# Flamingo stack, two layers, one core: layer 0's scores and values for eight heads in one visit, with a new order of the steps

## What is computed

```
x = x + tanh(g_xattn[0]) * xattn0(layernorm(x), ctx)   # 16 heads of 64
x = x + tanh(g_ffn[0])   * ffn0(layernorm(x))          # 8 experts, gate by softmax and threshold
x = x + tanh(g_xattn[1]) * xattn1(layernorm(x), ctx)   # 16 heads of 16
x = x + tanh(g_ffn[1])   * ffn1(layernorm(x))          # top 2 of 8, first two batches' 512 tokens

xattn0:  q = (x @ Wq.T).reshape(b, nq, H, DH);  k, v likewise from ctx
         sim  = einsum('bihd,bjhd->bhij', q, k) * SCALE
         attn = softmax(sim)
         out  = einsum('bhij,bjhd->bihd', attn, v) @ Wo.T + bo
```

## Time and profile before

| | |
|---|---|
| median of 3 runs | 3825.88 us |
| lowest to highest | 3822.79 to 3827.25 us |
| the profiled execution | 3827.74 us |
| its span, first to last instruction | 3826.0 us |
| mean granted PE clock over the span | 0.985 |
| PE busy | 3723.1 us (97%) |
| DVE busy | 2669.2 us (70%) |
| ACT busy | 1749.8 us (46%) |
| POOL busy | 1340.4 us (35%) |

### The profile page before, as it was taken

One profiled execution on the slowest core, in us unless ns is written; L12 is line 12 of the kernel. 1 busy time (PEld: TensorE's weight loads), 2 busy tenths in 40 slices (PEclk: granted clock), 3 DMA queues, 4 the chain that ended last, 5 costly groups with the idle time before them and its releaser, 6 DMA issues.

```text
span 3826.0 us, 96464 instructions
## 1 busy us (share of the span) xinstructions
PE 3723.1 (97%) x34836; PEld 2979.5 (78%) x34836; DVE 2669.2 (70%) x5726; ACT 1749.8 (46%) x3369; POOL 1340.4 (35%) x1301
## 2 busy tenths in 40 slices
PE   6999999999999999999999999999999999999959
PEld 4787878878878878787887887887888788788745
DVE  4676776777677677677777767767767777776646
ACT  4445445444444444544544444444454454444411
POOL 3334333333333433433333343343343333334300
PEclk8999999999999999999999999999999999999969
DMA  2000000000000000000000000000000000000001
GB/s 90 14 17 9 15 16 10 14 16 13 11 16 13 12 15 16 9 15 16 11 13 16 13 11 16 13 12 15 16 9 15 16 12 13 16 13 11 13 29 55
DMA packets 58914, 64.80 MB, mean 17 GB/s; under 512 B 5344, under 2 KB 55808, under 8 KB 58240
## 3 DMA queue, kind: packets, MB, share of 16 engines
q10 hardware_dynamic: 34688, 32.52, 2.9%
q1 hardware_dynamic: 24192, 31.81, 2.5%
HBM read 47.01 MB, written 17.30 MB: 17 GB/s over the span
## 4 chain that ended last, share of the span: by engine, by line
PE 84%; DVE 11%; issue 2%; POOL 2%; DVEq 1%; ACT 1%; DMA 0%; POOLq 0%; SPq 0%; ACTq 0%
PE g L693 25%; PE g L699 14%; PE scores L693 10%; PE scores L795 6%; PE g L853 6%; DVE xn L1048 4%; PE g L762 4%; PE g L862 3%; PE scores L846 3%; DVE y_nm L1126 3%; PE scores L827 3%; PE g L713 3%; PE scores L799 2%; PE g L773 1%; POOL y_rstd L437 1%
## 5 line engine op out<-in xcount | busy, mean ns | idle before, releaser
L623 ACT ACTIVATE prob<-scores 120x1024 f32<-120x1024 f32 x512 | 510.2, 1022 | 499.0 <-PE scores L799 327.4
L1187 DVE SCALAR_TENSOR_TENSOR x<-g,lg_w,x 128x256 f32<-128x256 f32 x1024 | 483.4, 482 | 61.1 <-PE g L693 36.1
L490 POOL TENSOR_TENSOR q_lo<-an,q_hi 128x512 fp32r<-128x512 f32 x256 | 328.5, 1284 | 341.3 <-ACT q_hi L654 341.3
L541 ACT CAST q_hi<-g 128x512 fp32r<-128x512 f32 x256 | 150.0, 586 | 582.7 <-PE g L693 582.6
L693 PE MATMUL g<-ew_hi,yT_hi 128*128 128x512 f32 x1024 | 412.3, 403 | 0.0
L693 PE MATMUL g<-ew_lo,yT_hi 128*128 128x512 f32 x1024 | 401.8, 392 | 0.0
L693 PE MATMUL g<-ew_hi,yT_lo 128*128 128x512 f32 x1024 | 399.9, 390 | 0.0
L435 POOL TENSOR_TENSOR y_rstd<-y_mv,eps 128x2 f32<-128x2 f32 x128 | 25.0, 195 | 1051.1 <-DVE y_mv L1043 1051.1
L1126 DVE TENSOR_REDUCE x_nm<-g 128x4 f32<-128x480 f32 x512 | 310.5, 648 | 102.3 <-PE g L762 102.3
L1126 DVE TENSOR_REDUCE y_nm<-g 128x4 f32<-128x480 f32 x512 | 301.0, 650 | 109.5 <-PE g L773 109.5
L1091 DVE TENSOR_TENSOR an<-g,inv 128x512 f32<-128x512 f32 x256 | 176.5, 690 | 239.3 <-ACT inv L644 155.7
(11 more groups left out here) (209 smaller groups left out, 9900.4 us busy)
## 6 DMA issues: line engine op xcount, KB each, us to landing
x_in<-in_x ACTq DMA_DIRECT2D x64, 256.0 KB, 2.9
out<-y_x SPq DMA_DIRECT2D x64, 256.0 KB, 2.1
ctx_in<-in_ctx ACTq DMA_DIRECT2D x128, 120.0 KB, 2.5
wk_s<-in_gu SPq DMA_DIRECT2D x8, 512.0 KB, 3.5
wk_s<-in_wk SPq DMA_DIRECT2D x1, 1024.0 KB, 5.1
prob<-in_wq SPq DMA_DIRECT2D x1, 1024.0 KB, 7.7
wv_s<-in_wv SPq DMA_DIRECT2D x1, 1024.0 KB, 10.3
vx<-in_wo SPq DMA_DIRECT2D x8, 128.0 KB, 7.9
```

The lines of the kernel that those rows point to most:

```text
L490: g.tensor_tensor(q[1][:, 2 * h:2 * h + 2, :], an[:, 2 * (h % 2):2 * (h % 2) + 2, :], q[0][:, 2 * h:2 * h + 2, :].bitcast(F32), ALU.subtra ...
L541: a.copy(dst, ring.bank(job)[:, 0:cols]).then_inc(done.sem, 1)
L623: a.activation(prob[:, e % 2].rearrange("p o u s -> p (o u s)"), scores[0:NK, banks, :].rearrange("p o c -> p (o c)"), ACT.Exp, scale=scal ...
L1187: ins = v.scalar_tensor_tensor(out=x1[:, t, :], in0=ring.bank(Y_FFN[j])[:, o * D:(o + 1) * D], scalar=lg_w[:, t, 2 * n + o:2 * n + o + 1], ...
```

## The change

A visit of `x_st` now makes the scores of two quads (eight heads): the first quad of the pair goes to banks 0 and 1 of `scores`, the second to banks 2 and 3. There are two visits instead of four. A visit of `x_pv` makes the sums of eight heads into one ring bank and then the values of its two quads into two further ring banks, so it has three jobs in the ring. The two visits of ACT to invert work on 512 columns each, read the sums from the ring bank and empty it. `pv` is no longer used for the sums. The ring has 56 jobs instead of 54 in a round, so the bank of nearly every job moves. `ORDER` is new throughout.

```diff
-            each = {"n_max": 2, "y_max": ROWS4}.get(name, 1)
+            each = {"n_max": 2, "y_max": ROWS4, "x_pv": 3}.get(name, 1)
...
-X_PV = [("x_pv", g) for g in range(QUADS)]
+X_SUM = [("x_pv", 3 * h) for h in range(2)]
+X_PV = [("x_pv", 3 * (g // 2) + 1 + g % 2) for g in range(QUADS)]
...
+            def x_st(i, h):
+                for g in (2 * h, 2 * h + 1):
+                    x_scored.wait(act, i, g + 1)
+                    if h == 1:
+                        ring.full(act, i, X_PV[g - 2])
+                    exp(g, slice(2 * (g % 2), 2 * (g % 2) + 2), SCALE0, x_probs)
...
+            def x_pv(i, h):
+                ring.full(act, i, X_SUM[h])
+                ring.has_emptied(a.activation(inv[:, h, :], ring.bank(X_SUM[h])[:], ACT.Ln), X_SUM[h])
+                ring.empty(act, i, X_SUM[h])
+                a.activation(inv[:, h, :], inv[:, h, :], ACT.Exp, scale=-1.0).then_inc(x_recip.sem, 1)
...
+                if h == 1:
+                    x_probs.wait(pe, i, 2)
+                for g in (2 * h, 2 * h + 1):
+                    x_qlo.wait(pe, i, g + 1)
+                    scores_of_quad(g, lambda rows, p: both(kT, rows, p, ALL),
+                                   lambda rows, p: both(q, rows, p, ALL), x_nmT).then_inc(x_scored.sem, 1)
...
+                x_probs.wait(pe, i, 2 * h + 2)
+                ring.to_fill(pe, i, X_SUM[h])
+                for u in range(2):
                     for j in range(4):
+                        ins = t_.matmul(ring.bank(X_SUM[h])[32 * j:32 * j + 32, u * S:(u + 1) * S], ones[0:NK, :],
+                                        prob[:, u, j % 2, j // 2, :], start=True, stop=True)
+                ring.has_filled(ins, X_SUM[h])
+                for g in (2 * h, 2 * h + 1):
+                    ring.to_fill(pe, i, X_PV[g])
```

The head of the order, from the first step of a round, before and after:

```diff
-    ("x_st", 0), ("y_k", 0), ("y_ffn", 0), ("n_load", 0), ("z_hi", 1), ("n_stat", 0), ("y_ffn", 1), ("n_norm", 0),
+    ("n_load", 0), ("x_st", 0), ("z_hi", 1), ("y_v", 0), ("y_ffn", 0), ("x_st", 1), ("x_pv", 0), ("n_stat", 0),
+    ("y_ffn", 1), ("x_mul", 0), ("x_hi", 0), ("x_mul", 1), ("n_norm", 0), ("y_ffn", 2), ("y_ffn", 3), ("y_ffn", 4),
...
```

More of the change, by code:

```diff
@@ L50 @@
 ORDER = (
-    ("x_st", 0), ("y_k", 0), ("y_ffn", 0), ("n_load", 0), ("z_hi", 1), ("n_stat", 0), ("y_ffn", 1), ("n_norm", 0),
[L52 to L60, removed]
+    ("n_load", 0), ("x_st", 0), ("z_hi", 1), ("y_v", 0), ("y_ffn", 0), ("x_st", 1), ("x_pv", 0), ("n_stat", 0),
+    ("y_ffn", 1), ("x_mul", 0), ("x_hi", 0), ("x_mul", 1), ("n_norm", 0), ("y_ffn", 2), ("y_ffn", 3), ("y_ffn", 4),
+    ("x_hi", 1), ("y_ffn", 5), ("y_ffn", 6), ("y_ffn", 7), ("n_tr", 0), ("y_stat3", 0), ("x_mul", 2), ("x_pv", 1),
+    ("x_hi", 2), ("y_norm3", 0), ("x_mul", 3), ("y_k", 0), ("n_ctx", 0), ("y_res", 0), ("x_hi", 3), ("z_out", 0),
+    ("p_load", 0), ("y_tr3", 0), ("n_k", 0), ("y_q", 0), ("n_k", 1), ("x_out", 0), ("y_max", 0), ("x_out", 1),
+    ("x_out", 2), ("y_max", 1), ("x_out", 3), ("p_stat", 0), ("p_norm", 0), ("n_q", 0), ("n_q", 1), ("y_maxt", 0),
+    ("y_maxt", 1), ("n_q", 2), ("n_q", 3), ("n_max", 0), ("p_tr2", 0), ("y_st", 0), ("n_max", 1), ("p_gate", 0),
+    ("n_max", 2), ("n_v", 0), ("p_lg", 0), ("n_maxt", 0), ("y_st", 1), ("y_pv", 0), ("y_mul", 0), ("n_max", 3),
+    ("p_wt", 0), ("n_v", 1), ("y_pv", 1), ("n_maxt", 1), ("y_mul", 1), ("p_ctx", 0), ("n_res", 0), ("p_eb", 0),
+    ("y_hi", 0),
 )
@@ L228, in flamingo_stack @@
         prob = prob_rows[0:NK]
-        an, inv = sb("an", [P, 4, S]), sb("inv", [P, 2, S])
+        an, inv = sb("an", [P, 4, S]), sb("inv", [P, 2, 2 * S])
         x1 = sb("x1", [P, T, D])
@@ L794, in scores_of_quad @@
                             rows = slice(64 * o, 64 * o + 64)
-                            t_.matmul(scores[0:NK, o, cols], keys(rows, p)[a], queries(rows, p)[b],
+                            t_.matmul(scores[0:NK, 2 * (g % 2) + o, cols], keys(rows, p)[a], queries(rows, p)[b],
                                       start=a + b == 0, stop=False)
@@ L798, in scores_of_quad, with x_st @@
                         rows = slice(64 * o, 64 * o + 64)
-                        ins = t_.matmul(scores[0:NK, o, cols], ident_r[rows, p:p + 1].broadcast_to([64, NK]),
+                        ins = t_.matmul(scores[0:NK, 2 * (g % 2) + o, cols], ident_r[rows, p:p + 1].broadcast_to([64, NK]),
                                         nmT[rows, :], start=False, stop=True)
                 return ins
-            def x_st(i, g):
+            def x_st(i, h):
                 if first(i):
@@ L833, in y_st, with x_pv @@
                 ins.then_inc(y_scored.sem, 1)
-            def x_pv(i, g):
-                x_probs.wait(pe, i, g + 1)
-                if g == 0:
+            def x_pv(i, h):
+                if h == 0:
                     if first(i):
@@ L869, in x_out @@
                 if c == 0:
-                    x_logged.wait(pe, i, 3)
+                    x_probs.wait(pe, i, QUADS)
                 if first(i):
@@ L1087, in x_mul @@
                 ring.full(dve, i, X_PV[g])
-                x_recip.wait(dve, i, g + 1)
+                x_recip.wait(dve, i, g // 2 + 1)
                 if g >= 2:
```

45 lines of the change are left out of this document (8 added, 37 removed).

## The result

The changed kernel takes 3866.2 us (median of four runs, 3863.0 to 3866.4), the kernel before 3826.6 us beside it: a ratio of 1.0106, 95% interval 1.0091 to 1.0121. It is slower, by 40 us where 13 had been forecast. The time lies inside the predicted range, but above the 3829 to 3858 us of the forecast's own case.

A forecast was written before the change was run, and what follows sets the result against it. PE, busy 996 of 1000 us, was taken as the bound. Terms of -0.32, -0.12, +0.08, +0.37 and +0.20 gave +0.21 us a round, times 64 +13 us: 3839 us, range 3802 to 3890.

The forecast's parts named there:

- the forecast's own case: Whole kernel: all terms together, about +0.05 to +0.5 us a round, 3829 to 3858 us; chance 0.45.
- (a): PE's scores: double visits enter and leave once, which saves merges, gaps and a slow first matmul, 0.66 us a round.
- (b): PE's sums and values: an added exit to experts and an entry of their own cost 0.32 us a round.
- (c): Transposes `p_tr2`: more PE work covers DVE's normalisation, so the wait shrinks from 0.38 to about 0.27, -0.12 us a round.
- (d): `n_v` 1 and `n_v` 0: late DVE transpose, and a bank of the second `n_max` reduction coming level; together +0.08 us.
- (e): `y_ffn` 2, behind the sums: PE waits for ACT's Ln to empty their bank, +0.37 us a round with restart.
- (f): `y_ffn` 3: PE waits for DVE's `x_mul` 0, which follows the additions of `y_ffn` 1, +0.20 us a round with restart.
- first double visit: First scores of a round: waits for nobody, its banks 2 and 3 having been read long before; no cost.
- The port: Rival: POOL's low part delays DVE's second normalisation at `y_norm3`; PE waits 0.9 us more a round, 3896 us; chance 0.12.
- Covered after all: Rival: Ln and `x_mul` 0 arrive in time for `y_ffn` 2 and 3; -0.36 us a round, 3803 us; chance 0.28.
- Even: Rival: `y_ffn` waits at lower bounds or `p_tr2` wait gone; -0.2 to +0.1 us a round, about 3824 us; chance 0.15.
- POOL's wait for the store: `y_res` on POOL waits for the same round's store, leaving about 1 us before `x_out` 1; no cost counted.

The follow-up runs named there:

- e3: The changed kernel with the second pair of exponentials behind the first Ln and Exp, and both products ahead of the first experts' additions: 3815.4 us, ratio 0.9982.
- e11: The kernel before with the orders of waits of e10 and nothing else: 3818.2 us, ratio 0.9985.
- e9: e3 with the first scores' wait for the bank released last put at the end of their waits: 3808.2 us, ratio 0.9956.
- e1: The changed kernel with the second visit's two exponentials issued behind the first Ln and Exp on ACT: 3861.1 us, ratio 1.0097.
- e2: The changed kernel with DVE's products `x_mul` 0 and 1 ahead of its additions of `y_ffn` 1: 3866.4 us, ratio 1.0116.
- e10: e9 with the wait released last also put last in the transposes and at every job of the ring: 3804.8 us, ratio 0.9948.
- e5: The changed kernel with the steps from `p_stat` to the round's end in the old order, `n_k` 1 staying in the first part: 3992.0 us, ratio 1.0441.

## Why the prediction had the sign right and the size too small

It said +0.21 us a round and the runs show +0.65. What it said would happen did: both new waits, at the two jobs named. But the time lies above the bounds of its own case, and is inside the range only because that was drawn wide enough for the rivals. The bounds were to hold as long as the terms don't all err the same way, and four of the five lines erred towards slower. By its own steps:

| step | predicted | measured |
|---|---|---|
| (a), (b) switches | -0.32 | -0.35, as the remainder |
| (c) `p_tr2` | -0.12 | -0.05 |
| (d) `n_v` 1 and the gate region | +0.08 | +0.22 |
| (e), (f) `y_ffn` 2 and 3 | +0.57 | +0.73 |
| first double visit | 0 | +0.10 |
| sum | +0.21 | +0.65 |

**(a), (b)** The one direct reading is the double visit, 2.08 us twice over, as worked out. The rest of the term was not isolated by a run; -0.35 is what the other lines leave, so its agreement is worth no more than they are.

**(e), (f)** The mechanism was right, and so were the starts: Ln of 512 columns took 0.60 (0.59 was taken from a copy), and `y_ffn` 2 and 3 started within 0.05 us of the forecast. The Trainium skill, page "ScalarE: Activation LUTs", section "What ACT_TABLE_LOAD costs", gives 186 ns + 0.833 ns for each element for an ACTIVATE with immediate scale and bias, which would be 0.61 us for 512. The trace agrees, with 0.60. Mis-sized was what a restart costs. Between `y_ffn` 1 and 4 the changed kernel takes 1.75, 1.69 and 1.50 us; e3 takes 1.49, 1.36 and 1.36. A job behind a restart is 1.49 or 1.50, one deep inside a stream 1.36: 0.14 for each restart, and 0.09 was counted for both together. So 0.73 is 0.26 and 0.19 of waiting (0.32 and 0.16 predicted) and twice 0.14. The sample job of the earlier trace rows, 1.39, is the first of 512 columns behind twelve matmuls of 256, and its distances hid this.

**(c)** Between 1000 and 3000 us the idle time ahead of these transposes went from 7.3 us (shown under e11) to 5.7:

```profile
L706 PE MATMUL g<-ident,xn 128*128 128x128 f32 x420 | 64.8, 277 | 5.7 <-DVE xn L1041 5.7
```

That is -0.05 a round. At one place of the changed kernel, DVE's pair, `n_max` 0 and `p_tr2`:

```profile
1971.51 2.68 DVE L1041 TENSOR_SCALAR xn<-x,y_mv,y_rstd 128x256 f32<-128x256 f32 x2 [1.09 <-POOL y_rstd L436]
...
1973.54 0.60 PE L755 MATMUL g<-kmx,q_hi 128*128 128x240 f32 x4
...
1974.32 0.65 PE L706 MATMUL g<-ident,xn 128*128 128x128 f32 x4 [0.18 <-DVE xn L1041]
```

`n_max` 0 takes 0.45, so 0.33 of the 0.78 is wait, against 0.38 before. DVE's pair is 0.04 us longer than in the earlier trace rows and takes back some of the cover. And PE starts 0.13 us behind the pair's end (1974.19) here as there: part of the wait is no lateness of DVE but the order of the waits, 0.10 as e11 shows for the kernel before.

**(d)** The step named both places and priced the first. `n_v` 0 waits 0.11 (four matmuls at 0.43 are 1.72, and 1979.67 - 1977.85 is 1.82) and `n_max` 2 0.08, because DVE has four reductions of 2.47 us in a row with only `p_gate` of PE between; `n_v` 1 waits 0.03 more. That the reduction "comes level" was the failing phrase: level already costs a tenth.

**The first double visit** was said to wait for nobody. Its banks for scores were indeed free, but it waits for the ring's banks of `n_maxt`, as the visit before did, and the change turned the order of those waits round. That step looked at what is waited for and not at the order in which it is asked: +0.10, and e9 gives back 0.08 of it.

**The rivals.** *The port* is out. Of the changed kernel, the pair of `y_norm3` and POOL's low part:

```profile
1953.52 0.74 DVE L1041 TENSOR_SCALAR xn<-x,y_mv,y_rstd 128x256 f32<-128x256 f32 x2 [0.28 <-POOL y_rstd L436]
```

```profile
1953.97 1.45 POOL L489 TENSOR_TENSOR q_lo<-an,q_hi 128x512 fp32r<-128x512 f32 x1 [0.48 <-ACT q_hi L647]
```

DVE was first by 0.45 us, not by 0.1, and ran at its full pace; POOL, which became ready during its second operation, took 1.45 instead of 1.28 us. These rows agree with the rule that the prediction quotes from the Trainium skill, page "SBUF — State Buffer", section "SBUF: two separate sides". *Covered after all* needed Ln by S+4.15, and it ended at S+4.42. But e3 reaches this case by two moves and gives 3815 us, against the 3803 worked out for it, for the same reasons as above: (c), (d) and the first visit. *Even* asked for smaller waits than there were. POOL's wait for the store, foreseen as harmless, is there (88.2 us in 63 rounds), and POOL ends no wait of PE.

## What to carry to other kernels

When a change makes two waits in one chain, price them together and test them together: e1 and e2 would each have been dropped as worthless, and together they are worth 0.71 us a round, some 45 us. Merging visits moves the last release of a bank; look again at every wait of the merged step, and put the one that comes last at the end of the row, then see whether the next wait of the chain takes the gain back, as in e10. And count the restart with the wait: 0.14 us here, as against waits of 0.26 and 0.19.

## What the runs showed of the hardware

Waits of one matmul that are already satisfied are not free. With the last-released one at the head of three, the scores start 0.22 to 0.23 us behind the release; with it in the middle (the kernel before) 0.12, with it at the end 0.14 in e9 and 0.08 in e10. So two satisfied waits behind it cost about 0.1 us, and what stands ahead of the three waits matters too, by 0.06 from e9 to e10. The Trainium skill, page "Advanced Engine Details and Errata", section "Network/Comms", gives 50 to 100 ns for a sequencer to read a semaphore; as an estimate from that figure, two such reads at the low end would be the 0.1 us measured. The Trainium skill, page "Perfetto Trace Analysis", section "Identifying Dependency Chains", says that an instruction which waits for several engines may have others ahead of it that hold the further waits. None of the runs tells the two waits apart.

A stream of 512-column matmuls has a settling cost besides the visible first distance (0.34 instead of 0.23): the first job of a stream takes 1.49 to 1.50 us, and later ones 1.36. Some 0.03 of the 0.14 lies in the distances after the first. Why these are longer is open; no run tried it.

A pair of DVE operations beside POOL takes a time that depends on who is first. The pair of `y_norm3` took 0.74 us ahead of POOL, and that of `p_norm` 2.68 with POOL at work from its start. `n_norm`'s pair took 1.72, and its two operations, with POOL's low part, tell why:

```profile
1943.01 0.40 DVE L1041 TENSOR_SCALAR xn<-x_in,x_mv,x_rstd 128x256 f32<-128x256 f32 x1
```

```profile
1943.23 1.35 POOL L489 TENSOR_TENSOR q_lo<-an,q_hi 128x512 fp32r<-128x512 f32 x1 [5.75 <-ACT q_hi L647]
```

```profile
1943.33 1.40 DVE L1041 TENSOR_SCALAR xn<-x_in,x_mv,x_rstd 128x256 f32<-128x256 f32 x1
```

The first started ahead of POOL and ran its 0.40 us. The second started behind it and ended at 1944.73, 0.15 us after POOL's operation (1944.58). No wait of PE came of it.

A wait of 1.94 us can cost more than itself: in e5 the granted clock fell to 0.50 behind it in one round of three, and such a round was 1.56 us longer.
